# Attention kernel on one core: probability blocks through DRAM, two stores and four loads a head

## The chip, the cores and the metric

The kernel runs on one core of one Trainium2 chip. The metric is the device time of one execution in microseconds. Before the change three timed executions took 833.21, 831.81 and 833.38 us; their median is 833.21 us.

A core has a TensorE (PE) for matrix products, a VectorE (DVE), a ScalarE (ACT) and a GpSimd (POOL), and a SyncE (SP) that here issues every DMA. Each engine runs its own instructions in order and waits on semaphores for the others. A DMA is issued in SP's queue and lands later.

## The reference, cut to what matters

One layer of cross attention and one linear layer with 4-bit weights and a low-rank addition. There are 8 batches (B) of 128 queries and 128 keys, width 512, 32 heads (H) of 128.

```python
x = rmsnorm(layernorm(x)) * ln_weight
q, k, v = x @ w_q.T, ctx @ w_k.T, ctx @ w_v.T        # 32 heads of 128
score = einsum('bqhd,bkhd->bhqk', q, k) + position_bias
score = where(mask, softmax(where(mask, score, -inf)), 0)
x = x0 + layernorm(x0) + einsum('bhqk,bkhd->bqhd', score, v) @ w_out.T
h = layernorm(x)
out = x + h @ W.T + 2 * (h @ W_a @ W_b)              # W decoded from 4-bit codes
```

## The kernel before, in words

Every large product is made from operands split into a high and a low part (fp32r), three products for one, on PE (line 1184). After a setup, in which head 0's scores are made too, a loop of seven passes and an unrolled eighth treats four heads a pass (G = 4, functions odd_head and even_head of each engine); the last head, 31, stands behind it. All orders are written out by hand.

One head h goes through these steps. PE makes the scores of 8 batches into the banks s_ps (line 1220). DVE adds the bias and takes the maximum (lines 992, 994). ACT takes the exponential with a sum (line 652) into p_blocks, whose free axis is ordered as block of 32 keys, batch, key within the block. DVE makes a factor for each row (lines 999, 1001), ACT multiplies by it (normalise, line 603). DVE then transposes every 32x32 block in place (turn_blocks, line 1009, two instructions of 128x512; p_turned_done counts them).

For `pT`, the probabilities with keys on the partitions, the blocks must also change places: block row i, column k goes to row k, column i. That is the work of `move_blocks` on SP (line 342), 16 DMAs of 32 partitions by 1 KB within SBUF. When they have landed (pT_loaded), PE uses pT for the attention of head h while it is at head h+1 (attend, line 1226). Since pT is single, the move waits until the attention of head h-1 is done (attn_done); since p_blocks is single, ACT waits for the whole move before the exponential of the next head (the wait on pT_loaded in `exps`, at the first half).

Head 0 goes another way before the loop. ACT writes its exponentials ordered by batch (by_batches, the same memory under the name last_pT). PE transposes the 8 tiles with the identity (line 1326), between the two halves of head 1's queries, and DVE copies the result into pT (line 1087). DVE's last step of the first split, of ctx_sum[3] into ctx_lo (split_first 7, line 895), stands ahead of that copy. PE waits for it (`ctx_lo_done, SPLITS`) before it enters the loop with the scores of head 1.

At the end, head 31 is transposed by PE as well; its ACT copy into last_pT, which is the memory of p_blocks, waits for the move of head 30.

SP's queue holds, behind each move, the loads of later weights: k_raw and wo_raw for the next pair of heads, q_raw for head h+3, pos_raw for head h+2, and in the second head of each pass the storing of a decoded slice and the loading of the next.

Of the kernel before, what the change touches and what calls it, by code (L numbers as in the profile page):

```python
# [6 lines left out]
P = 128  # L7
B = 8
# [3 lines left out]
H = 32  # L12
# [6 lines left out]
HB = B // 2  # L19
Q = 32  # L20
# [41 lines left out]
SPLITS = 8  # L62

EARLY_LORA = 3
TURN_BEFORE = (5, 7)
FFN_TRANSPOSE_BEFORE = 5
WARM_UP = 4
# [11 lines left out]
def halves(h):  # L79
    return range(h * HB, (h + 1) * HB)  # L80
# [15 lines left out]
def xattn_ffn(nc, x_d, ctx_d, mask_d, lnw_d, q_d, k_d, pos_d, wo_d, wv_d, codes_d, absmax_d, wa_d, wb_d, out_d):  # L96
    lora_d = nc.dram_tensor("lora_dram", (GROUPS, P, SLICE), f32, kind="Internal").ap()
    ffn_d = nc.dram_tensor("ffn_dram", (GROUPS, P, SLICE), f32, kind="Internal").ap()
    with ExitStack() as ctx:
        def sb(name, shape, dt=f32):  # L100
            return ctx.enter_context(nc.sbuf_tensor(name, shape, dt))

        def sem(name):
            return ctx.enter_context(nc.semaphore(name))
# [134 lines left out]
        decode_moved = sem("decode_moved")  # L239
        ffn_loaded = sem("ffn_loaded")  # L240
        last_ffn_loaded = sem("last_ffn_loaded")
        pT_loaded = sem("pT_loaded")
        stored = sem("stored")

# [35 lines left out]
        p_done = sem("p_done")  # L280
        p_turned_done = sem("p_turned_done")
        turned = sem("turned")
        first_turned = sem("first_turned")
        last_pT_done = sem("last_pT_done")
        attn_done = sem("attn_done")
        attn_hi_done = sem("attn_hi_done")
# [28 lines left out]
        def _(sp):  # L315
# [20 lines left out]
                sp.wait_ge(decoded, g + 1)  # L336
                sp.dma_start(ffn_d[g], level[:, :]).then_inc(decode_moved, 16)

            def move_blocks(keys):
                for k in keys:  # L340
                    for i in range(NQ):
                        sp.dma_start(pT[Q * k:Q * (k + 1), i, :, :],  # L342
                                     p_blocks[Q * i:Q * (i + 1), k, :, :]).then_inc(pT_loaded, 16)

            sp.dma_start(wa, wa_d).then_inc(lora_loaded, 16)
            sp.dma_start(wb, wb_d).then_inc(lora_loaded, 16)
# [30 lines left out]
            load_q(2)  # L377
            sp.wait_ge(bias_done, 1)
            load_pos(2, 0)
            sp.wait_ge(q_lo_done, 3)  # L380
            load_q(3)

# [2 lines left out]
            def group(g, last):  # L385
                for j in range(1, G if last else G + 1):
                    h = G * g + j
                    final = last and j == G - 1
                    m = 2 * g + (j + 1) // 2
                    if j == 1:  # L390
                        if last:

                            sp.wait_ge(wv_lo_done, PRODUCTS * GROUPS)
                            sp.wait_ge(decode_moved, 80 * (GROUPS - 1) + 64)
                            sp.dma_start(wv_raw[:, 0:C - 1, :].rearrange("p c (g s) -> p (c g) s", g=2),
                                         ffn_d[0:2 * (C - 1)].rearrange("g p s -> p g s")).then_inc(ffn_loaded, 16)
                        else:
                            sp.wait_ge(wv_lo_done, PRODUCTS * (g + 1))
                            sp.dma_start(wv_raw[:, :, :], wv_d[g + 1]).then_inc(wv_loaded, 16)
                    if not (last and j + 2 >= G):  # L400
                        sp.wait_ge(bias_done, h + 1)
                        load_pos(h + 2, j % 2)
                    if not final:
                        sp.wait_ge(p_turned_done, 2 * h + 1)
                        sp.sem_inc(sp_passed, 1)
                        sp.wait_ge(attn_done, 2 * h)
                        move_blocks((0, 1))
                        sp.wait_ge(p_turned_done, 2 * h + 2)
                        move_blocks((2, 3))
                    if j % 2 and not last:  # L410
                        sp.wait_ge(k_lo_done, PRODUCTS * (m + 1))
                        load_k(m + 1)
                    if j == 1 or (j == 3 and not last):
                        for i in range(2):
                            sp.wait_ge(wo_lo_done, h + i)
                            load_wo(h + 1 + i, i)
                    if not last:
                        sp.wait_ge(q_lo_done, h + 3)
                        load_q(h + 3)
                        if j == 2:  # L420
                            store_ffn(g)
                            load_codes(g + 1)
                    elif j == 2:
                        store_ffn(g)
                        sp.wait_ge(decode_moved, 80 * GROUPS)
                        sp.dma_start(wv_raw[:, C - 1, :].rearrange("p (g s) -> p g s", g=2),
                                     ffn_d[2 * (C - 1):2 * C].rearrange("g p s -> p g s")).then_inc(last_ffn_loaded, 16)
# [173 lines left out]
        def _(act):  # L601
# [44 lines left out]
            def exps(h, hf, out):  # L646
                act.wait_ge(max_done, 2 * h + hf + 1)
                if hf == 0 and out is by_blocks and not (isinstance(h, int) and h == 0):

                    act.wait_ge(pT_loaded, 16 * NQ * NQ * h)  # L650
                for b in halves(hf):
                    e = act.activation(out(b), p[:, b, :].rearrange("p (k c) -> p k c", c=Q), ACT.Exp,  # L652
                                       bias=neg_max[:, b:b + 1], accum_out=prob_sum[:, b:b + 1])
# [1 line left out]

            def by_blocks(b):
                return p_blocks[:, :, b, :]

            def by_batches(b):
                return last_pT[:, b, :].rearrange("p (k c) -> p k c", c=Q)  # L660

            def in_place(b):
                return p[:, b, :].rearrange("p (k c) -> p k c", c=Q)
# [102 lines left out]


            for hf in range(2):
                exps(0, hf, by_batches)
            for hf in range(2):  # L770
                normalise(0, hf, by_batches)
            act.wait_ge(lora_stored, 16 * C)
            copy_first_values(6)
            copy_first_values(7)
# [85 lines left out]
            for i in range(2):  # L860
                split_wo(i, PAIRS, last_wo_hi)

            act.wait_ge(pT_loaded, 16 * NQ * NQ * (H - 1))
            for hf in range(2):
                act.wait_ge(turned, hf + 1)
                copy(last_pT[:, hf * HB:(hf + 1) * HB, :], s_ps[hf][:, :, :]).then_inc(last_pT_done, 1)
# [26 lines left out]
        def _(dve):  # L893
# [184 lines left out]
            scale_rows(0, 0)  # L1078
            residual(HB)
            scale_rows(0, 1)  # L1080
            for b in range(HB + 1, B):
                residual(b)
            split_first(7, ctx_lo[:, 4, :, :], ctx_sum[3], ctx_hi[:, 4, :, :])

            for hf in range(2):
                dve.wait_ge(first_turned, hf + 1)
                dve.tensor_copy(pT[:, :, hf * HB:(hf + 1) * HB, :],
                                s_ps[hf][:, :, :].rearrange("p b (i c) -> p i b c", c=Q)).then_inc(pT_loaded, 8 * NQ * NQ)
            dve.sem_inc(p_turned_done, 2)
            split_q(2)  # L1090

            def odd_head(g, j, last):
# [84 lines left out]
        def _(pe):  # L1177
# [141 lines left out]
            scores(0, 1)  # L1319
            for b in (6, 7):  # L1320
                first_values(b)
            queries(1, 0, next_queries[0])
            for hf in range(2):
                pe.wait_ge(p_done, hf + 1)
                for i, b in enumerate(halves(hf)):
                    t = pe.transpose(s_ps[hf][:, i, :], last_pT[:, b, :], ident[:, :])
                t.then_inc(first_turned, 1)
            queries(1, 1, next_queries[1])

            pe.wait_ge(ctx_lo_done, SPLITS)  # L1330
            pe.wait_ge(pT_loaded, 16 * NQ * NQ)

            def odd_head(g, j, last):

# [10 lines left out]
                key_product(m, 1, key_slot(j, 1))  # L1345
                if j == 1:
                    pe.wait_ge(values_added, 2 * ADDS * (g + 1))
                pe.wait_ge(pT_loaded, 16 * NQ * NQ * h)
                for hf in range(2):
                    pe.wait_ge(biased, 2 * h + hf + 1)  # L1350
                    attend(j - 1, hf, s_flat(hf), moved)
# [14 lines left out]
            def even_head(g, j, last):  # L1366
# [8 lines left out]

                pe.wait_ge(keys_copied, COPIES * (m + 1))
                queries(h + 1, 0, query_bank(j, 0))
                pe.wait_ge(pT_loaded, 16 * NQ * NQ * h)
                for hf in range(2):
                    pe.wait_ge(biased, 2 * h + hf + 1)  # L1380
                    attend(j - 1, hf, s_flat(hf), moved)
# [39 lines left out]
            for b in range(B):  # L1421
# [11 lines left out]
                if b >= 4:  # L1433
                    pe.wait_ge(out_added, B * (PAIRS - 2) + b - 3)
                output(b, wo_hi, wo_lo)
            pe.wait_ge(pT_loaded, 16 * NQ * NQ * (H - 1))
            for hf in range(2):
                attend(G - 2, hf, w_ps[hf][:, :], moved)
                pe.wait_ge(last_pT_done, hf + 1)
# [67 lines left out]
```

## Time and profile before

| | before |
|---|---|
| median of three | 833.21 us |
| lowest, highest | 831.81, 833.38 us |
| profiled execution | 831.71 us |
| its span | 829.9 us |
| PE busy | 824.1 us, 99% |
| POOL busy | 535.3 us, 65% |
| DVE busy | 447.5 us, 54% |
| ACT busy | 445.6 us, 54% |
| share of the DMA queue's packets | 24.9% |
| granted TensorE clock | 1.00 |

The span is the time from the first to the last instruction of the program; the execution has 1.8 us around it. A row of the timeline has the start in us from the span's start, the length in us, the engine, the line, the operation, the tile written and the tiles read, the shapes, how many were merged, and in brackets the idle time ahead of it with what ended it. Matmul rows overlap: the pace is the distance between starts, not the length.

### The profile page before, as it was taken

Reading aid. Unit: us, or ns where it says so; the run is one execution under the profiler, and the core shown is the slowest. Engines: PE = TensorE matmul, PEld = TensorE weight load, DVE = VectorE, ACT = ScalarE, POOL = GpSimd, SP = SyncE. Lnnn points to the kernel's source line nnn. Section 1 sums busy time; section 2 is a strip of 40 time slices with the busy share of each in tenths; the row PEclk is TensorE's granted clock in tenths of the full one; section 3 lists DMA queues with packets and bytes.
Section 4 is the critical chain, followed back from the end, with each engine's and each line's share of the span. In section 5 each row is a group of like instructions: output and inputs, shape, how many; then the busy total and the mean of one; then the engine's idle time right before and its main releaser. Section 6 shows DMA issues by size and latency. Waiting matters only on the chain.

```text
span 829.9 us, 15761 instructions
## 1 busy us (share of the span) xinstructions
PE 824.1 (99%) x4702; PEld 720.3 (87%) x4702; DVE 447.5 (54%) x754; ACT 445.6 (54%) x1297; POOL 535.3 (65%) x556
## 2 busy tenths in 40 slices
PE   9999999999999999999999999999999999999998
PEld 6888888988899888988889888998889888898886
DVE  5785655355634656245553556346562455636683
ACT  5766474464726555364644647355553646447632
POOL 0576778467875778756785578757787567855440
PEclk9999999999999999999999999999999999999999
DMA  8212332122211323113221222113230232311102
GB/s 326 90 42 90 107 94 68 54 92 66 93 36 58 98 68 97 26 69 98 79 89 54 92 66 92 38 55 97 69 96 24 71 98 68 104 41 51 46 13 89
DMA packets 50357, 64.46 MB, mean 78 GB/s; under 512 B 10752, under 2 KB 36480, under 8 KB 49312
## 3 DMA queue, kind: packets, MB, share of 16 engines
q1 hardware_dynamic: 50336, 64.20, 24.9%
q8 instruction: 10, 0.16, 0.1%
q14 instruction: 11, 0.09, 0.0%
HBM read 44.24 MB, written 4.19 MB: 58 GB/s over the span
## 4 chain that ended last, share of the span: by engine, by line
PE 94%; DVE 2%; ACT 2%; SPq 1%; DMA 0%; issue 0%; POOL 0%; POOLq 0%; ACTq 0%
PE w_ps L1184 44%; PE o_ps L1184 35%; PE s_ps L1220 6%; PE s_ps L1226 6%; SPq L342 1%; ACT p_blocks L652 1%; DVE stats L901 1%; DVE resid L1017 1%; PE s_ps L1184 1%; ACT p_blocks L603 1%; PE s_ps L1250 0%; PE o_ps L1250 0%; PE w_ps L1286 0%; PE w_ps L1241 0%; PE w_ps L1247 0%; DMA pT<-p_blocks 0%
## 5 line engine op out<-in xcount | busy, mean ns | idle before, releaser
L531 POOL TENSOR_SCALAR picked<-codes 128x256 f32<-128x256 int32 x112 | 124.3, 1110 | 19.2 <-POOL level L534 15.6
L496 POOL TENSOR_TENSOR p<-pos_raw,mask_add 128x1024 f32<-128x1024 f32 x32 | 69.6, 2175 | 103.1 <-ACT p_blocks L652 102.8
L652 ACT ACTIVATE p_blocks<-p,neg_max 128x128 f32<-128x128 f32 x248 | 96.1, 389 | 48.4 <-DVE neg_max L994 44.0
L534 POOL TENSOR_TENSOR level<-level,picked 128x256 f32<-128x256 f32 x112 | 90.6, 809 | 20.9 <-POOL picked L531 20.9
L468 POOL TENSOR_TENSOR ring_lo<-k_raw,ring_hi 128x256 fp32r<-128x256 f32 x105 | 76.5, 740 | 30.2 <-ACT ring_hi L603 27.3
L603 ACT ACTIVATE ring_hi<-k_raw 128x256 fp32r<-128x256 f32 x105 | 38.8, 414 | 101.0 <-POOL k_raw L458 101.0
L1017 DVE TENSOR_TENSOR resid<-o_ps,resid 128x512 f32<-128x512 f32 x102 | 68.7, 686 | 44.7 <-PE o_ps L1184 44.5
L1184 PE MATMUL w_ps<-ctx_hi,ring_hi 128*128 128x512 f32 x210 | 84.7, 403 | 0.0
L1184 PE MATMUL w_ps<-ctx_hi,ring_lo 128*128 128x512 f32 x210 | 82.1, 391 | 0.0
L1184 PE MATMUL w_ps<-ctx_lo,ring_hi 128*128 128x512 f32 x210 | 81.7, 389 | 0.0
L603 ACT ACTIVATE p_blocks<-p_blocks,row_scale 128x128 f32<-128x128 f32 x248 | 77.2, 391 | 1.1 <-DVE row_scale L1001 1.1
L1184 PE MATMUL o_ps<-wo_hi,attn_hi 128*128 128x512 f32 x180 | 70.2, 390 | 0.0
L1184 PE MATMUL o_ps<-wo_hi,attn_lo 128*128 128x512 f32 x180 | 70.1, 389 | 0.0
L1184 PE MATMUL o_ps<-wo_lo,attn_hi 128*128 128x512 f32 x180 | 70.0, 389 | 0.0
L992 DVE TENSOR_TENSOR p<-s_ps,p 128x512 f32<-128x512 f32 x62 | 42.5, 686 | 41.8 <-PE s_ps L1220 41.8
L1220 PEld LDWEIGHTS s_ps<-kT,qT 128*128 128x128 f32 x496 | 59.8, 191 | 1.9
L1220 PE MATMUL s_ps<-kT,qT 128*128 128x128 f32 x496 | 60.4, 275 | 0.0
L1226 PEld LDWEIGHTS s_ps<-pT,v 128*128 128x128 f32 x480 | 58.2, 191 | 2.3
L1009 DVE STREAM_TRANSPOSE p_blocks<-p_blocks 128x512 f32<-128x512 f32 x60 | 39.1, 691 | 36.7 <-ACT p_blocks L603 36.7
L1226 PE MATMUL s_ps<-pT,v 128*128 128x128 f32 x480 | 58.4, 275 | 0.0
L895 DVE TENSOR_TENSOR attn_lo<-s_ps,attn_hi 128x512 fp32r<-128x512 f32 x62 | 40.9, 680 | 31.1 <-ACT attn_hi L603 31.1
L984 DVE TENSOR_TENSOR v<-w_ps,v 128x512 f32<-128x512 f32 x21 | 14.5, 692 | 76.7 <-PE w_ps L1184 76.7
(229 smaller groups left out, 2289.8 us busy)
## 6 DMA issues: line engine op xcount, KB each, us to landing
pT<-p_blocks SPq DMA_DIRECT2D x480, 32.0 KB, 1.8
k_raw<-k_dram SPq DMA_DIRECT2D x16, 512.0 KB, 3.5
wv_raw<-wv_dram SPq DMA_DIRECT2D x8, 1024.0 KB, 4.8
q_raw<-q_dram SPq DMA_DIRECT2D x32, 256.0 KB, 3.7
wo_raw<-wo_dram SPq DMA_DIRECT2D x32, 256.0 KB, 4.0
resid<-x_dram SPq DMA_DIRECT2D x2, 1024.0 KB, 12.6
pos_raw<-pos_dram SPq DMA_DIRECT2D x32, 64.0 KB, 3.8
out_dram<-resid SPq DMA_DIRECT2D x8, 256.0 KB, 2.0
```

What stands on the lines that cost most here:

```text
L468: return pool.tensor_tensor(out, whole, hi.bitcast(f32), ALU.subtract)
L496: pool.tensor_tensor(p[:, :, :], pos, mask_add[:, :, :], ALU.add).then_inc(bias_done, 1)
L531: then(pool.tensor_scalar((level if code == 0 else picked)[:, :], codes[:, :], float(code), NF4[code], match, ALU.mult))
L534: then(pool.tensor_tensor(level[:, :], level[:, :], picked[:, :], ALU.add))
L603: return act.activation(out, in_, ACT.Copy, **kw)
L652: e = act.activation(out(b), p[:, b, :].rearrange("p (k c) -> p k c", c=Q), ACT.Exp, bias=neg_max[:, b:b + 1], accum_out=prob_sum[:, b:b + 1])
L895: return dve.tensor_tensor(out, whole, hi.bitcast(f32), ALU.subtract)
L992: dve.tensor_tensor(p[:, bs, :], banks[hf][:, :, :], p[:, bs, :], ALU.add).then_inc(biased, 1)
L1017: dve.tensor_tensor(resid[:, b, :], bank, resid[:, b, :], ALU.add).then_inc(out_added, 1)
L1184: mm = pe.matmul(out, l, r, start=opens and i == 0, stop=closes and i == n - 1, skip_group_check=True)
L1220: s = pe.matmul(banks[hf][:, i, :], qT[:, at], kT[:, slot, at], start=True, stop=True)
L1226: o = pe.matmul(out[:, i * L:(i + 1) * L], v[:, b, j * DH:(j + 1) * DH], by_keys(b), start=True, stop=True)
```

## The change

The stores write p_blocks, two columns of blocks at a time, into a new DRAM tensor blocks_dram; the loads read it back with the block index on the other side, one load for each 32 partitions of pT, all four block columns at once. SP waits for a store's landing (blocks_stored, one semaphore for each pair) before it loads from it. ACT's wait in `exps` and at the end is now for the two stores. Head 0 goes the same way: its exponentials are written by blocks, DVE turns them (turn_blocks(0), ahead of three residual steps and the last split), SP moves them; PE's 8 transposes and DVE's two copies are gone.

```diff
+STORE = 16
+LOADS = 16 * NQ
+    blocks_d = nc.dram_tensor("blocks_dram", (2, P, 2, B, Q), f32, kind="Internal").ap()
-            def move_blocks(keys):
-                for k in keys:
-                    for i in range(NQ):
-                        sp.dma_start(pT[Q * k:Q * (k + 1), i, :, :],
-                                     p_blocks[Q * i:Q * (i + 1), k, :, :]).then_inc(pT_loaded, 16)
+            def move(h):
+                first = isinstance(h, int) and h == 0
+                for pair in range(2):
+                    sp.wait_ge(p_turned_done, 2 * h + pair + 1)
+                    if pair == 0 and not first:
+                        sp.sem_inc(sp_passed, 1)
+                        sp.wait_ge(pT_loaded, LOADS * h)
+                    sp.dma_start(blocks_d[pair], p_blocks[:, 2 * pair:2 * pair + 2, :, :]).then_inc(blocks_stored[pair], STORE)
+                if not first:
+                    sp.wait_ge(attn_done, 2 * h)
+                    sp.sem_inc(sp_passed, 1)
+                for pair in range(2):
+                    sp.wait_ge(blocks_stored[pair], STORE * (h + 1))
+                    for k in range(2):
+                        at = 2 * pair + k
+                        sp.dma_start(pT[Q * at:Q * (at + 1), :, :, :],
+                                     blocks_d[pair, :, k, :, :].rearrange("(i r) b c -> r i b c", i=NQ)).then_inc(pT_loaded, 16)
...
             load_pos(2, 0)
+            move(0)
...
-                        sp.wait_ge(p_turned_done, 2 * h + 1)
-                        sp.sem_inc(sp_passed, 1)
-                        sp.wait_ge(attn_done, 2 * h)
-                        move_blocks((0, 1))
-                        sp.wait_ge(p_turned_done, 2 * h + 2)
-                        move_blocks((2, 3))
+                        move(h)
...
-                    act.wait_ge(pT_loaded, 16 * NQ * NQ * h)
+                    for pair in range(2):
+                        act.wait_ge(blocks_stored[pair], STORE * h)
...
-                exps(0, hf, by_batches)
+                exps(0, hf, by_blocks)
...
             scale_rows(0, 1)
+            turn_blocks(0)
             for b in range(HB + 1, B):
                 residual(b)
             split_first(7, ctx_lo[:, 4, :, :], ctx_sum[3], ctx_hi[:, 4, :, :])
-            for hf in range(2):
-                dve.wait_ge(first_turned, hf + 1)
-                dve.tensor_copy(pT[:, :, hf * HB:(hf + 1) * HB, :],
-                                s_ps[hf][:, :, :].rearrange("p b (i c) -> p i b c", c=Q)).then_inc(pT_loaded, 8 * NQ * NQ)
-            dve.sem_inc(p_turned_done, 2)
...
-            queries(1, 0, next_queries[0])
             for hf in range(2):
-                pe.wait_ge(p_done, hf + 1)
-                for i, b in enumerate(halves(hf)):
-                    t = pe.transpose(s_ps[hf][:, i, :], last_pT[:, b, :], ident[:, :])
-                t.then_inc(first_turned, 1)
-            queries(1, 1, next_queries[1])
+                queries(1, hf, next_queries[hf])
             pe.wait_ge(ctx_lo_done, SPLITS)
-            pe.wait_ge(pT_loaded, 16 * NQ * NQ)
+            pe.wait_ge(biased, 2)
...
-                pe.wait_ge(pT_loaded, 16 * NQ * NQ * h)
+                pe.wait_ge(pT_loaded, LOADS * h)
```

PE's order between the halves of head 1's queries and the loop (the branch), before:

```order
L1184 MATMUL w_ps<-xn_hi,q_lo 128x512
L1326 MATMUL s_ps<-ident,p_blocks 128x128 [waits p_done]
L1326 MATMUL s_ps<-ident,p_blocks 128x128 x3
L1326 MATMUL s_ps<-ident,p_blocks 128x128 [waits p_done]
L1326 MATMUL s_ps<-ident,p_blocks 128x128 x3
L1184 MATMUL w_ps<-xn_hi,q_hi 128x512 [waits q_lo_done]
...
L1411 UNCONDITIONAL_BRANCH [waits pT_loaded,ctx_lo_done]
```

and now:

```order
L1193 MATMUL w_ps<-xn_hi,q_lo 128x512
L1193 MATMUL w_ps<-xn_hi,q_hi 128x512 [waits q_lo_done]
L1193 MATMUL w_ps<-xn_lo,q_hi 128x512
...
L1415 UNCONDITIONAL_BRANCH [waits biased,ctx_lo_done]
```

The 8 transposes are gone, and the two waits for p_done; the wait for ctx_lo_done at the loop's entry stays.

DVE's order at the same place, from the second half's row factors on, before:

```order
L999 RECIPROCAL recip<-prob_sum 128x4 [waits exp_done]
L1001 TENSOR_TENSOR row_scale<-recip,row_valid 128x4 [waits recip_done]
L944 TENSOR_SCALAR resid<-resid,ln_scale,ln_shift 128x512 [waits staged] x3
L895 TENSOR_TENSOR ctx_lo<-wv_raw,ctx_hi 128x1024 [waits ctx_hi_done]
L1087 COPY pT<-s_ps 128x4x128 [waits first_turned] x2
L895 TENSOR_TENSOR q_lo<-q_raw,q_hi 128x512 [waits q_hi_done]
```

and now:

```order
L1013 RECIPROCAL recip<-prob_sum 128x4 [waits exp_done]
L1015 TENSOR_TENSOR row_scale<-recip,row_valid 128x4 [waits recip_done]
L1023 STREAM_TRANSPOSE p_blocks<-p_blocks 128x512 [waits p_done]
L1023 STREAM_TRANSPOSE p_blocks<-p_blocks 128x512
L958 TENSOR_SCALAR resid<-resid,ln_scale,ln_shift 128x512 [waits staged] x3
L909 TENSOR_TENSOR ctx_lo<-wv_raw,ctx_hi 128x1024 [waits ctx_hi_done]
L909 TENSOR_TENSOR q_lo<-q_raw,q_hi 128x512 [waits q_hi_done]
```

Two transposes of blocks with a wait for p_done now stand ahead of the three residual steps and of the split into ctx_lo; the two copies into pT are gone.

SP's order in a head of the loop, before:

```order
L342 DMA pT<-p_blocks 32x256 [waits p_turned_done,attn_done]
L342 DMA pT<-p_blocks 32x256 x7
L408 REGISTER_ALU
L342 DMA pT<-p_blocks 32x256 [waits p_turned_done]
L342 DMA pT<-p_blocks 32x256 x7
```

and now:

```order
L353 DMA blocks_dram<-p_blocks 128x512 [waits pT_loaded]
L348 REGISTER_ALU
L353 DMA blocks_dram<-p_blocks 128x512 [waits p_turned_done]
L358 REGISTER_ALU [waits attn_done]
L361 DMA pT<-blocks_dram 32x4x256 [waits blocks_stored0]
L361 DMA pT<-blocks_dram 32x4x256
L361 DMA pT<-blocks_dram 32x4x256 [waits blocks_stored1]
L361 DMA pT<-blocks_dram 32x4x256
```

Six issues stand where sixteen stood, with two waits for a landing among them. Head 0's six stand in the same order ahead of the loop.

## Rows read from the trace of the kernel before

**Rows 1.** The page, part 1: busy us, share of the span, instructions.
```profile
PE 824.1 (99%) x4702; PEld 720.3 (87%) x4702; DVE 447.5 (54%) x754; ACT 445.6 (54%) x1297; POOL 535.3 (65%) x556
```

**Rows 2.** The waits of PE: us in total, times, longest us.
```profile
PE w_ps L1247 <- POOL ident L447: 1.6, 1, 1.6
PE o_ps L1220 <- ACT qT L603: 0.7, 1, 0.7
PE o_ps L1184 <- DVE xn_lo L895: 0.4, 1, 0.4
```

**Rows 3.** The timeline of PE, head 0's transposes to its attention: start, length.
```profile
58.46 0.40 PE L1184 MATMUL w_ps<-xn_hi,q_lo 128*128 128x512 f32 x1
58.69 1.04 PE L1326 MATMUL s_ps<-ident,p_blocks 128*128 128x128 f32 x8
59.49 0.47 PE L1184 MATMUL w_ps<-xn_hi,q_hi 128*128 128x512 f32 x1
59.80 0.39 PE L1184 MATMUL w_ps<-xn_lo,q_hi 128*128 128x512 f32 x1
...
62.34 2.01 PE L1220 MATMUL s_ps<-kT,qT 128*128 128x128 f32 x16
...
66.94 1.95 PE L1226 MATMUL s_ps<-pT,v 128*128 128x128 f32 x16
```

**Rows 4.** The timeline of DVE, at head 0, head 1 and head 30.
```profile
54.62 1.99 DVE L1001 TENSOR_TENSOR row_scale<-recip,row_valid 128x4 f32<-128x4 f32 x1
56.54 1.45 DVE L944 TENSOR_SCALAR resid<-resid,ln_scale,ln_shift 128x512 f32<-128x512 f32 x3
57.91 1.22 DVE L895 TENSOR_TENSOR ctx_lo<-wv_raw,ctx_hi 128x1024 fp32r<-128x1024 f32 x1
...
71.86 1.30 DVE L1009 STREAM_TRANSPOSE p_blocks<-p_blocks 128x512 f32<-128x512 f32 x2 [1.96 <-ACT p_blocks L603]
...
763.99 0.69 DVE L994 TENSOR_REDUCE neg_max<-p 128x4 f32<-128x512 f32 x1
```

**Rows 5.** The timeline of ACT, at head 0, head 2 and head 30.
```profile
56.65 1.28 ACT L603 ACTIVATE p_blocks<-p_blocks,row_scale 128x128 f32<-128x128 f32 x4 [1.10 <-DVE row_scale L1001]
...
84.39 0.40 ACT L652 ACTIVATE p_blocks<-p,neg_max 128x128 f32<-128x128 f32 x1 [2.37 <-DMA pT<-p_blocks]
...
764.99 0.40 ACT L652 ACTIVATE p_blocks<-p,neg_max 128x128 f32<-128x128 f32 x1 [2.02 <-DMA pT<-p_blocks]
```

**Rows 6.** The timeline of POOL at head 0.
```profile
54.46 2.14 POOL L496 TENSOR_TENSOR p<-pos_raw,mask_add 128x1024 f32<-128x1024 f32 x1 [0.80 <-ACT p_blocks L652]
...
60.29 0.74 POOL L458 TENSOR_TENSOR k_raw<-k_raw 128x256 f32<-128x256 f32 x1 [0.18 <-POOL ring_lo L468]
61.21 0.74 POOL L458 TENSOR_TENSOR k_raw<-k_raw 128x256 f32<-128x256 f32 x1 [0.18 <-POOL k_raw L458]
```

**Rows 7.** The timeline of SP's queue, the move of head 1.
```profile
72.66 10.45 SPq L342 DMA_DIRECT2D pT<-p_blocks  x16
```

**Rows 8.** DMA issues: count, KB each, median us to landing.
```profile
pT<-p_blocks SPq DMA_DIRECT2D x480, 32.0 KB, 1.8
...
resid<-x_dram SPq DMA_DIRECT2D x2, 1024.0 KB, 12.6
...
lora<-lora_dram SPq DMA_DIRECT2D x8, 128.0 KB, 3.0
...
ffn_dram<-level SPq DMA_DIRECT2D x8, 128.0 KB, 2.6
```

**Rows 9.** SP's lines 337 and 342: issue ns min/median/max, first and last start.
```profile
L337 SPq DMA_DIRECT2D ffn_dram<-level x8: 364/370/581, 102.1 to 782.2; - x8
L342 SPq DMA_DIRECT2D pT<-p_blocks x480: 508/590/1270, 72.7 to 781.5; - x160
```

**Rows 10.** The timeline of PE at head 2's attention step and at head 31's scores.
```profile
85.74 1.95 PE L1226 MATMUL s_ps<-pT,v 128*128 128x128 f32 x16
...
772.11 1.13 PE L1220 MATMUL o_ps<-kT,qT 128*128 128x128 f32 x8 [0.69 <-ACT qT L603]
```

More of the change, by code:

```diff
@@ L241, in xattn_ffn @@
         last_ffn_loaded = sem("last_ffn_loaded")
+        blocks_stored = [sem(f"blocks_stored{i}") for i in range(2)]
         pT_loaded = sem("pT_loaded")
@@ L282, in xattn_ffn @@
         turned = sem("turned")
-        first_turned = sem("first_turned")
         last_pT_done = sem("last_pT_done")
@@ L657, in by_blocks @@
                 return p_blocks[:, :, b, :]
-            def by_batches(b):
-                return last_pT[:, b, :].rearrange("p (k c) -> p k c", c=Q)
             def in_place(b):
@@ L768, in _ @@
             for hf in range(2):
-                exps(0, hf, by_batches)
+                exps(0, hf, by_blocks)
             for hf in range(2):
-                normalise(0, hf, by_batches)
+                normalise(0, hf, by_blocks)
             act.wait_ge(lora_stored, 16 * C)
@@ L861, in _ @@
                 split_wo(i, PAIRS, last_wo_hi)
-            act.wait_ge(pT_loaded, 16 * NQ * NQ * (H - 1))
+            for pair in range(2):
+                act.wait_ge(blocks_stored[pair], STORE * (H - 1))
             for hf in range(2):
@@ L1377, in even_head @@
                 queries(h + 1, 0, query_bank(j, 0))
-                pe.wait_ge(pT_loaded, 16 * NQ * NQ * h)
+                pe.wait_ge(pT_loaded, LOADS * h)
                 for hf in range(2):
@@ L1435, in _ @@
                 output(b, wo_hi, wo_lo)
-            pe.wait_ge(pT_loaded, 16 * NQ * NQ * (H - 1))
+            pe.wait_ge(pT_loaded, LOADS * (H - 1))
             for hf in range(2):
```

## The prediction

> **What bounds the kernel now.** I read the busy shares first, then the waits of PE, then the timelines of the engines around head 0 and around the last heads, and last what SP issues and when it lands. PE is busy 824.1 us of a span of 829.9 us, the next engine 65% [rows 1]. The list of all that PE waited for has three entries, 1.6, 0.7 and 0.4 us [rows 2]; the first is before the first product of the kernel. So the time is PE's own work, instruction after instruction, and an edit counts in two ways only: by work taken from PE, or by a wait of PE made or removed. No entry names the move of the blocks. Whatever the 16 transfers cost SP, PE has not waited for one in any of the heads. The reader is to see in the timeline of PE that the pace is 0.23 us a product of 512 columns (58.46 to 58.69) and that the rows follow each other without idle time [rows 3].
>
> **Work taken from PE.** The 8 transposes of head 0 start at 58.69 and the next product at 59.49, so 0.80 us; the product behind them takes 0.31 us to the next start (59.49 to 59.80) where others take 0.23 [rows 3]. Together 0.88 us, if nothing takes the place.
>
> **What takes the place: the entrance of the loop.** PE reaches the wait for ctx_lo_done now at 62.34 [rows 3], and the split that it waits for ended at 57.91 + 1.22 = 59.13 [rows 4], 3.2 us early. After the change PE is there at 62.34 - 0.88 = 61.46. DVE is later. The row factors end at 54.62 + 1.99 = 56.61 [rows 4], the normalising of the second half at 56.65 + 1.28 = 57.93 [rows 5], and only then may the turn of the blocks start, 1.30 us for the two by the row at 71.86; then three residual steps, 1.45 us, then the split, 1.22 us [rows 4]. That is 57.93 + 1.30 + 1.45 + 1.22 = 61.90, less about 0.1 for overlaps of rows: 61.8. So PE waits 0.35 us at the least. The split reads two tensors of SBUF, and at that time POOL now works on the key sums, 60.29 to 61.03 and from 61.21 [rows 6]. What such a meeting costs shows at 54.62: DVE's factors of 128x4, an operation with two inputs, took 1.99 us and ended at 56.61, when POOL's bias, 54.46 to 56.60, ended [rows 4, 6]. DVE would be ready for the split at about 60.6, POOL's sum runs until 61.03, so 0.4 us more: the split ends at 62.25 and PE is released near 62.3. I take a wait of 0.8 us. Ends: 0.35 us (no meeting), and 1.6 us (POOL first with both sums, until 61.95). The Trainium skill, "SBUF — State Buffer", on the engine side's shared port, says that DVE's operations with two SBUF inputs and GpSimd's exclude each other for a whole instruction; by that rule the wait is the 0.8, without it the 0.35, and the row of 1.99 us agrees with the rule.
>
> Who is behind the wait: the scores of head 1, and with them DVE's bias, ACT's exponential and all of PE. ACT's queries of head 1 come 0.88 us earlier, so they do not hold the scores. POOL's next sums slip by up to 1 us. Their first use is later by several products, so I count them at nothing.
>
> **Head 0's blocks.** They are needed by PE at 66.94 now [rows 3], that is 66.06 with the transposes gone and 66.9 with the 0.8 us wait. The turn ends at 57.93 + 1.30 = 59.2, SP's second store is issued by 59.2 + 0.1 + 0.37 = 59.7 (0.37 from the store of a decoded slice) [rows 9]. A store to DRAM lands after 2.6 us by the row of ffn_dram [rows 8]: 62.3; the first pair's by 61.7. Four loads follow. An issue costs between 0.37 and 0.59 us [rows 9], so the last is issued between 63.2 and 64.1; it lands after 3.0 us by the row of lora, which has the same 128 KB [rows 8]: 66.2 to 67.1. That is even with 66.9. I take no further wait, as the middle, 66.65, is before it. The ends are 1.8 us a landing as for moves within SBUF [rows 8], which gives 64.7 and nothing to wait for, and issues of 1.27 us [rows 9], which gives 61.7 + 4 x 1.27 + 3.0 = 69.8, a wait of 2.9 us more.
>
> A sentence apart: the Trainium skill, "DMA: Bandwidth & Descriptors", anatomy of one DMA, gives about 2.0 us fixed for each transfer plus its bytes over 436 GB/s (a fit for the GpSimd path), most of it for the receipt of the write, and DRAM as the slowest target; a chain of store and load then pays the fixed part twice, an estimate of 2.6 + 2.3 us, which speaks against this change. By it head 0's blocks would land at about 66.1. The measured 2.6 and 3.0 us say the same, a little more.
>
> **The heads of the loop.** SP issues 16 transfers from 72.66 for 10.45 us, and the last lands 1.8 us later [rows 7, 8]; PE needs them at 85.74 [rows 10]. Now the first store goes at the same time; the second is issued about 0.7 us after the first, lands at about 76.3; the loads are issued by 78.6 and landed by 81.6. The blocks come about 3 us earlier, and SP reaches its loads of weights about 4.5 us earlier. PE was not waiting, so both are worth nothing. ACT waited for the move twice before an exponential: at 84.39 and at 764.99 [rows 5]; now it waits for the stores, long landed. In head 2 PE has no wait behind it (rows 2 name none) and the gain is nothing. At head 30 it is on the path: behind the exponentials and the normalising ACT drains head 31's queries, and PE is idle 0.69 us for them at 772.11 [rows 10]. But the maximum that ACT also needs ended only at 763.99 + 0.69 = 764.68 [rows 4]; ACT would have started near 764.72. The gain is 0.27 us, not 2.02. It can't be under nothing or over 0.69. At the end ACT's copy of head 31 waits for head 30's move; PE used it without a wait, so nothing.
>
> **Sum.** -0.88 + 0.8 - 0.27 = -0.35 us. Against the profiled execution, 831.71 us, that is 831.36. The median is 833.21, and four executions of this kernel (with the profiled one) lie between 831.71 and 833.38 with a mean of 832.53. Median less sum is 832.9, mean less sum 832.2; I take the middle, 832.5 us. What a measurement can tell from no change is about 0.2%, 1.7 us; the sum is a fifth of that.
>
> **The rivals.**
> 1. Head 0's blocks are late and end PE's wait at 66.1 to 66.9, not ctx_lo. For: the two estimates overlap, and two landings stand in a chain where there was none. Price: a landing at 67.1 gives 0.2 us more, at 69.8 2.9 us more; so 832.7 to 835.4, most likely 833.2.
> 2. The change is a clean gain: DVE's split is not delayed by POOL (0.35 us), the blocks are early. -0.88 + 0.35 - 0.27 = -0.8 us, 832.0 us.
> 3. Faster by more than the resolution: PE's 0.88 us are all saved, and both late idle times, 0.69 and 0.4 us [rows 2], vanish since everything arrives early. -1.97 us: 830.8 us. Against it: the 0.4 us at the end wait for DVE's work that has nothing to do with the move, and the maximum at 764.68.
> 4. Slower: the round trip through DRAM is longer than the slack of the heads in the loop. The blocks of an odd head are turned at 71.86 + 1.30 = 73.16 and needed at 85.74, 12.6 us [rows 4, 10]. Issues take 0.4 + 4 x 0.59 = 2.8 us, so the two landings may take 9.8 us together; beyond that each us costs 1 us in 15 heads, and 0.12 us over is already 0.2%. Landings of 12.6 us occur, in the crowd of the first loads [rows 8]; with those it would be 15 x 15 us more. One us over, as a mark: 848 us. Against: in the loop ffn_dram and lora land in 2.6 and 3.0 us, 4 us inside the limit, and the queue's packets fill a quarter of the time.
>
> **How the numbers follow.** Forecast (-0.35) 0.48; rival 1 0.22; rival 2 0.15; rival 3 0.05; rival 4 0.05; something that no row shows, either way, 0.05. All of forecast, 1 up to a landing 1.7 us late, and 2 are within 0.2%; the spread of a median of three (1.6 us between lowest and highest) puts some of them outside. Faster 0.11, same 0.78, slower 0.11. The range, 831.0 to 834.8, takes in the sums from -0.8 to about +1.5 us and that spread; rivals 3 and 4 and the far end of 1 are left out.
>
> **What would show it.** Right: PE has 8 matmuls fewer; a new wait of PE, 0.5 to 1 us, before the first scores of head 1, ended by DVE's ctx_lo; the attention of head 0 starts near 66.9; the moves of a head take SP about 6 us in place of 10.5; ACT has no wait for the move at 84 and 765; PE's wait for ACT's qT near 772 is about 0.4 us. Wrong: PE waits for pT anywhere in the loop; a wait for pT at head 0 of over 1 us; no wait for ctx_lo at all; a PE wait at 772 that is gone or unchanged; a span more than 1.7 us away from 829.5.

## The result

| | before | after |
|---|---|---|
| median of 20 runs each, same chip | 832.52 us | 833.97 us |
| lowest, highest | 831.81, 833.43 | 833.04, 834.53 |
| ratio, 95% interval | | 1.0018 [1.0012, 1.0024] |
| profiled execution: span | 829.9 us | 831.3 us |
| first scores of head 0 to first scores of head 1 | 13.69 us | 15.01 us |

The change makes the kernel slower by 1.45 us, with 1.0 to 2.0 us inside the interval. The forecast was 832.5 us, no change. Against the 832.52 us of before in these runs the sum of the prediction, -0.35 us, was off by 1.8 us.

The page after, part 1, against [rows 1]:

```profile
PE 823.6 (99%) x4694; PEld 720.0 (87%) x4694; DVE 451.2 (54%) x754; ACT 445.8 (54%) x1297; POOL 535.9 (64%) x556
```

PE has 8 matmuls fewer and 0.5 us less work, and the span is longer: it waits. The waits of PE after, against [rows 2]:

```profile
PE s_ps L1229 <- DVE ctx_lo L909: 2.1, 1, 2.1
PE w_ps L1256 <- POOL ident L462: 1.6, 1, 1.6
PE o_ps L1229 <- ACT qT L618: 0.4, 1, 0.4
PE o_ps L1193 <- DVE xn_lo L909: 0.4, 1, 0.4
```

The first is new, and it is the wait that the prediction named, at 2.1 us in place of 0.8. The third is the one at head 31's scores, down from 0.7 to 0.4 as forecast. No wait is for pT. The timeline of PE after, against [rows 3] (line 1229 is the scores, line 1235 the attention):

```profile
61.70 0.39 PE L1193 MATMUL w_ps<-xn_hi,q_lo 128*128 128x512 f32 x1
64.17 2.05 PE L1229 MATMUL s_ps<-kT,qT 128*128 128x128 f32 x16 [2.08 <-DVE ctx_lo L909]
...
68.81 1.95 PE L1235 MATMUL s_ps<-pT,v 128*128 128x128 f32 x16
```

From the last product to the scores it is 2.47 us where 0.23 would do: a loss of 2.24 us. The timeline of DVE after, against [rows 4]:

```profile
58.48 1.31 DVE L1023 STREAM_TRANSPOSE p_blocks<-p_blocks 128x512 f32<-128x512 f32 x2 [1.35 <-ACT p_blocks L618]
59.71 2.30 DVE L958 TENSOR_SCALAR resid<-resid,ln_scale,ln_shift 128x512 f32<-128x512 f32 x3
61.93 1.78 DVE L909 TENSOR_TENSOR ctx_lo<-wv_raw,ctx_hi 128x1024 fp32r<-128x1024 f32 x1
```

The three residual steps took 2.30 us where they had taken 1.45, the split 1.78 where it had taken 1.22. What GpSimd did at that time, against [rows 6]:

```profile
59.89 0.92 POOL L483 TENSOR_TENSOR ring_lo<-k_raw,ring_hi 128x256 fp32r<-128x256 f32 x1 [2.78 <-ACT ring_hi L618]
60.99 0.74 POOL L473 TENSOR_TENSOR k_raw<-k_raw 128x256 f32<-128x256 f32 x1 [0.18 <-POOL ring_lo L483]
61.91 0.72 POOL L473 TENSOR_TENSOR k_raw<-k_raw 128x256 f32<-128x256 f32 x1 [0.18 <-POOL k_raw L473]
62.59 1.70 POOL L483 TENSOR_TENSOR ring_lo<-k_raw,ring_hi 128x256 fp32r<-128x256 f32 x1
```

GpSimd works through all of it, and its own key splits are longer as well, 0.92 and 1.70 us where they take 0.74. The chain of waits of the stretch, up to PE's scores at 64.17; each line has the start, the length and the piece of work:

```profile
58.48 1.31 DVE p_blocks L1023 x2
59.79 2.22 DVE resid L958 x3
62.01 1.71 DVE ctx_lo L909
63.72 0.44 issue
```

The chain runs through DVE for 5.2 us and has 0.44 us between DVE's end and PE's first product, in which PE's queue starts again. The moves themselves went well. SP's queue at head 1 after, against [rows 7], and what they took to land, against [rows 8]:

```profile
74.00 0.81 SPq L353 DMA_DIRECT2D blocks_dram<-p_blocks  x2
76.04 1.74 SPq L361 DMA_DIRECT2D pT<-blocks_dram  x4
```

```profile
blocks_dram<-p_blocks SPq DMA_DIRECT2D x62, 256.0 KB, 2.2
pT<-blocks_dram SPq DMA_DIRECT2D x124, 128.0 KB, 2.6
```

SP is done 3.8 us after it began, where it had taken 10.45 us. The differences along the two profiles: the setup up to the first scores of head 0 is 0.51 us longer (48.65 and 49.16), from there to head 1's scores it is +1.32 us, from there to head 31's scores -0.45 us (62.34 to 772.11, and 64.17 to 773.49), and the rest is equal. The 0.51 us are no part of the change: two further executions of the same changed kernel have 47.97 there (experiment 7).

### The profile page after: what moved, and what is told of

It is laid out like the page before. It is cut to its first block, busy times and chain, and to the rows that moved or that the text cites. A ratio compares the mean times of both kernels' runs of the same rounds, so it can differ in the third digit from the quotient of the medians.

```text
span 831.3 us, 15555 instructions
## 1 busy us (share of the span) xinstructions
PE 823.6 (99%) x4694; PEld 720.0 (87%) x4694; DVE 451.2 (54%) x754; ACT 445.8 (54%) x1297; POOL 535.9 (64%) x556
## 3 DMA queue, kind: packets, MB, share of 16 engines
HBM read 60.49 MB, written 20.45 MB: 97 GB/s over the span
## 4 chain that ended last, share of the span: by engine, by line
PE 95%; DVE 3%; ACT 1%; issue 0%; POOL 0%; POOLq 0%
PE w_ps L1193 45%; PE o_ps L1193 35%; PE s_ps L1229 6%; PE s_ps L1235 6%; ACT p_blocks L668 1%; DVE stats L915 1%; DVE resid L1031 1%; PE s_ps L1193 1%; PE s_ps L1259 0%; ACT p_blocks L618 0%; PE o_ps L1259 0%; PE w_ps L1295 0%; DVE ctx_lo L909 0%; DVE resid L958 0%; PE w_ps L1250 0%; PE w_ps L1256 0%
## 6 DMA issues: line engine op xcount, KB each, us to landing
resid<-x_dram SPq DMA_DIRECT2D x2, 1024.0 KB, 12.3
```

## The experiments

All ratios are to the kernel before in the same runs. The edits are to the changed kernel.

**1. The split ahead of the turn.**

```diff
             scale_rows(0, 1)
+            split_first(7, ctx_lo[:, 4, :, :], ctx_sum[3], ctx_hi[:, 4, :, :])
             turn_blocks(0)
             for b in range(HB + 1, B):
                 residual(b)
-            split_first(7, ctx_lo[:, 4, :, :], ctx_sum[3], ctx_hi[:, 4, :, :])
```

> The changed kernel with DVE's last split into ctx_lo put ahead of the turn of head 0's blocks, and the three residual steps behind it. Theory A (the time was lost by PE's wait for ctx_lo at the loop's entrance, 2.24 us from product to product, because DVE does the turn, three residual steps and only then the split): the wait is gone, head 0's blocks start as early as before, and what stays is the work taken from PE, -0.88 us, and -0.27 us at head 30: 1.1 us under the kernel before, ratio 0.9986. Rival B (the loop pays for the way through DRAM, and the wait only takes the place of another that would come): the time stays at 1.0 to 1.5 us over the kernel before, with a wait of PE for pT or k_lo in place of the one for ctx_lo.

Measured: 830.59 us, ratio 0.9984 [0.9975, 0.9993]. The waits of PE:

```profile
PE w_ps L1256 <- POOL ident L462: 1.6, 1, 1.6
PE o_ps L1229 <- ACT qT L618: 0.4, 1, 0.4
PE o_ps L1193 <- DVE xn_lo L909: 0.4, 1, 0.4
```

The wait for ctx_lo is gone and nothing has taken its place; DVE used the 1.4 us in which it waited for the normalising. The three residual steps still take 2.30 us there, but now nobody waits for them. This is theory A: 1.1 us under the kernel before expected, 1.4 us measured (832.01 in these runs). The order of the steps turns a loss into a gain.

**2. The loop alone through DRAM.** Head 0 by PE's transposes and DVE's copies as in the kernel before; the copies also tell the semaphores of the stores.

```diff
-            move(0)
...
-            turn_blocks(0)
...
+            for hf in range(2):
+                dve.wait_ge(first_turned, hf + 1)
+                dve.tensor_copy(pT[:, :, hf * HB:(hf + 1) * HB, :],
+                                s_ps[hf][:, :, :].rearrange("p b (i c) -> p i b c", c=Q)).then_inc(pT_loaded, LOADS // 2)
```

> Only the loop's moves go through DRAM; head 0 goes as in the kernel before (8 transposes on PE, copies by DVE). Theory A: the loop's part is worth -0.27 us at head 30 and nothing else, ratio 0.9997, PE's wait for qT 0.4 us instead of 0.7. Rival B: the loop's part is what costs, +1 us or more, ratio 1.0012 or more.

Measured: 831.47 us, ratio 0.9995 [0.9986, 1.0004]. PE's wait for qT is 0.4 us. The loop's part costs nothing and gains at most what was expected; rival B, 1.0012 or more, is outside the interval.

**3. Head 0 alone through DRAM.** The loop's 16 transfers back in place of the stores and loads.

```diff
+                if not first:
+                    sp.wait_ge(p_turned_done, 2 * h + 1)
...
+                            sp.dma_start(pT[Q * k:Q * (k + 1), i, :, :],
+                                         p_blocks[Q * i:Q * (i + 1), k, :, :]).then_inc(pT_loaded, 16)
```

> Only head 0 goes through DRAM; the loop moves its blocks by 16 transfers within SBUF as in the kernel before. Theory A: -0.88 us of transposes and +2.24 us of the wait for ctx_lo, so +1.4 us, ratio 1.0016, and PE waits 2.1 us before the first scores of head 1. Rival B: -0.9 to 0 us, since the costly part is not in it.

Measured: 834.08 us, ratio 1.0026 [1.0015, 1.0037], so +2.1 us. The waits of PE:

```profile
PE s_ps L1238 <- DVE ctx_lo L918: 2.1, 1, 2.1
PE o_ps L1238 <- ACT qT L629: 1.1, 1, 1.1
```

The whole loss is here, and the expected 1.4 us lie inside the interval. 0.4 us of the rest show in the second row: with the moves within SBUF head 31's scores waited 1.1 us, where the kernel before waited 0.7. The last 0.3 us are not explained; the clock does not show in them, since the three executions with a granted clock of 1.0 (median 834.06 us) are level with the five at 0.997 or 0.998 (834.13). Experiments 2 and 3 together settle which part of the change costs.

**4. GpSimd held back until the split is made.**

```diff
             make_bias(1)
+            pool.wait_ge(ctx_lo_done, SPLITS)
             start_of_pair(1, 1)
```

> The changed kernel, with GpSimd's first key split and key sums of the first pair held back until DVE has made the last split into ctx_lo. Theory A2 (DVE's residual steps and its split are stretched by GpSimd's work at the same time, 2.30 us for 1.45 and 1.78 for 1.22): they take 1.45 and 1.22 us again, ctx_lo is done 1.4 us earlier, and the whole is 1.3 us under the changed kernel, about level with the kernel before (ratio 1.0000), if the key splits, 2.5 us later, still come before their products. Rival (the lengths have another cause, such as the stores of the blocks that read SBUF at that time): the two lengths stay and so does PE's wait, ratio 1.0018 or more.

Measured: 834.52 us, ratio 1.0035 [1.0021, 1.0049]. The timeline of DVE:

```profile
59.32 1.42 DVE L959 TENSOR_SCALAR resid<-resid,ln_scale,ln_shift 128x512 f32<-128x512 f32 x3
60.66 1.22 DVE L910 TENSOR_TENSOR ctx_lo<-wv_raw,ctx_hi 128x1024 fp32r<-128x1024 f32 x1
```

The theory on the lengths holds: with GpSimd idle they are 1.42 and 1.22 us, although SP's stores of the blocks run at that time as before. The time did not follow. PE's two waits, and two of the products behind them:

```profile
62.32 1.15 PE L1230 MATMUL s_ps<-kT,qT 128*128 128x128 f32 x8 [0.64 <-DVE ctx_lo L910]
64.69 1.95 PE L1230 MATMUL s_ps<-kT,qT 128*128 128x128 f32 x8 [1.22 <-ACT qT L619]
66.87 0.63 PE L1194 MATMUL w_ps<-ctx_lo,ring_hi 128*128 128x512 f32 x1
67.30 0.63 PE L1194 MATMUL w_ps<-ctx_hi,ring_lo 128*128 128x512 f32 x1
```

ACT's draining of head 1's queries stands behind its copy of GpSimd's late key sum, and PE waited 1.22 us for it: my sentence "if the key splits still come before their products" had looked past the copy. Then the products ran at 0.43 us instead of 0.23. The stretches of PE there (the number after the engines' busy times is the granted clock):

```profile
64.00:66.20 2.20, 1.51 (x7) 1.51 (x8) 1.01 (x2) 1.16 (x3) 2.02 (x3) 0.70 0.00 0
66.20:68.50 2.30, 2.30 (x9) 1.86 (x8) 2.23 (x4) 1.84 (x8) 1.49 (x3) 0.55 0.46 132
```

The granted clock fell to the lower level, 1.2 GHz for 2.4, after two waits of together 1.9 us. All five executions of this kernel have a mean clock of 0.998.

**5. The split between the turn and the residual steps.**

```diff
             turn_blocks(0)
+            split_first(7, ctx_lo[:, 4, :, :], ctx_sum[3], ctx_hi[:, 4, :, :])
             for b in range(HB + 1, B):
                 residual(b)
-            split_first(7, ctx_lo[:, 4, :, :], ctx_sum[3], ctx_hi[:, 4, :, :])
```

> The changed kernel with DVE's order turn, split into ctx_lo, residual steps (instead of turn, residual steps, split). Theory A (PE waits for ctx_lo alone): the split ends about 61.0, before PE arrives at 61.9, and the time is that of the first experiment, 1.1 us under the kernel before, ratio 0.9986. Theory A3 (an operation of DVE with two SBUF inputs holds up a GpSimd operation, and ACT stands in order behind GpSimd): the split, 59.7 to 60.9, pushes GpSimd's key split of 59.89 to 60.9, its first key sum to 62.6, ACT's copy of it to 63.0 and ACT's draining of head 1's second half of queries to 63.5; PE then waits about 0.8 us for qT before the second four scores, in place of any wait for ctx_lo: 0.3 us under the kernel before, ratio 0.9996.

Measured: 831.47 us, ratio 0.9989 [0.9980, 0.9998]. DVE and GpSimd:

```profile
58.91 1.18 DVE L909 TENSOR_TENSOR ctx_lo<-wv_raw,ctx_hi 128x1024 fp32r<-128x1024 f32 x1
60.02 2.77 DVE L958 TENSOR_SCALAR resid<-resid,ln_scale,ln_shift 128x512 f32<-128x512 f32 x3
```

```profile
59.09 1.60 POOL L483 TENSOR_TENSOR ring_lo<-k_raw,ring_hi 128x256 fp32r<-128x256 f32 x1 [2.77 <-ACT ring_hi L618]
```

This time DVE began first and kept its length, and GpSimd's operation was the one stretched: its 0.74 us became 1.60, ending 0.6 us behind the end of the split at 60.09. The effect on PE is that of A3, a wait for qT, but of 0.4 us and not 0.8:

```profile
62.59 1.16 PE L1229 MATMUL s_ps<-kT,qT 128*128 128x128 f32 x8 [0.40 <-ACT qT L618]
```

The ratio stands between the two expectations and cannot tell them apart; the row can.

**6. PE's wait moved behind the branch.**

```diff
-            pe.wait_ge(ctx_lo_done, SPLITS)
             pe.wait_ge(biased, 2)
...
                 pe.wait_ge(attn_lo_done, 2 * (h - 1) + 2)
+                if j == 1:
+                    pe.wait_ge(ctx_lo_done, SPLITS)
                 scores(h, 0)
```

> The changed kernel, with PE's wait for ctx_lo_done moved from the branch at the loop's entrance to the place just before the scores in the loop body. DVE is as late as before. Theory A4 (PE starts 0.46 us after DVE's end instead of 0.05 to 0.13 as behind other waits because the branch and what follows it come after the wait): the wait shrinks from 2.08 to about 1.75 us, 0.35 us under the changed kernel, ratio 1.0014. Rival (the restart costs 0.4 us wherever the wait stands): the wait stays 2.1 us, ratio 1.0018.

Measured: 833.71 us, ratio 1.0016 [1.0007, 1.0025]. The split ended at 61.48 + 1.78 = 63.26 and PE began at 63.51:

```profile
61.48 1.78 DVE L909 TENSOR_TENSOR ctx_lo<-wv_raw,ctx_hi 128x1024 fp32r<-128x1024 f32 x1
```

```profile
63.51 2.75 PE L1229 MATMUL s_ps<-kT,qT 128*128 128x128 f32 x16 [1.88 <-DVE ctx_lo L909]
```

The restart took 0.25 us where it took 0.46. So about 0.2 us of it go with the place of the wait, at the branch; this rests on one profile, and the other half is not explained. In this execution the clock fell behind the wait (products at 0.43 us), and the interval of the ratio holds both expectations, so the time can't show 0.2 us.

**7. The changed kernel twice more.** No edit.

> The changed kernel as it is, one more profiled execution. Theory C (PE's wait of 2.1 us at the loop's entrance is close to what makes the granted clock fall, so that some executions pay for it twice): either as in the first profile (clock 1.0 throughout, first scores of head 1 to the attention of head 0 4.64 us) or a stretch of 3.4 us at half clock behind the wait, and that distance 6.2 us. Rival: the clock never falls there.

> As the one before, a third profiled execution of the changed kernel, with the same two outcomes: 4.64 us and clock 1.0, or 6.2 us with 3.4 us at half clock.

Measured: 833.54 and 833.47 us, spans 831.8 and 831.7 us. In both the clock fell. Scores and attention of the first of them, and its stretch behind the wait:

```profile
62.97 3.68 PE L1229 MATMUL s_ps<-kT,qT 128*128 128x128 f32 x16 [2.08 <-DVE ctx_lo L909]
...
69.25 1.95 PE L1235 MATMUL s_ps<-pT,v 128*128 128x128 f32 x16
```

```profile
62.00:64.00 2.00, 1.03 (x5) 1.04 (x6) 1.64 (x2) 0.04 (x1) 1.82 (x2) 0.77 0.50 151
64.00:66.00 2.00, 2.00 (x11) 2.00 (x11) 0.88 (x2) 0.72 (x2) 1.20 (x3) 0.50 0.38 140
```

Against the first profile of the same kernel:

```profile
62.00:64.00 2.00, 0.08 (x1) 0.00 (x0) 2.00 (x3) 1.24 (x3) 2.00 (x2) 1.00 0.67 205
64.00:66.00 2.00, 1.83 (x17) 1.84 (x17) 1.37 (x2) 0.55 (x2) 1.25 (x2) 1.00 0.37 68
```

69.25 - 62.97 = 6.28 us in place of 68.81 - 64.17 = 4.64: the same wait of 2.08 us costs 1.6 us more in two of three executions. In these two the setup was 1.19 us shorter (head 0's scores at 47.97 for 49.16), so the spans differ by 0.4 to 0.5 us only.

The record has the mean granted clock of each execution, and it tells how often this happens. A fall like this one loses 1.7 us (the clock is 0.77, 0.50 and 0.87 in the three stretches of 2 us from 62 to 68), 0.002 of 832 us, and so shows as 0.998. Of the 20 executions of the changed kernel in the result 16 have 0.998. The other four, at 0.999 and 1.0, are also the four fastest: their median is 833.31 us against 834.16, and the profiled execution, 833.04 us, is one of them. Over all the kernels in which PE waits 1.9 us or more there, in one wait or two (the changed kernel and experiments 3, 4 and 6) 35 of 46 executions have 0.998 or 0.997. Of the 135 executions on record with a clock without such a wait (72 of the kernel before, 63 of experiments 1, 2, 5, 9 and the stores twice and four times) none is under 0.999.

**8. The stores twice, four times, six times.** Each repetition waits for the one before; the kernel is that of experiment 1.

```diff
+                    for again in range(N):
+                        for pair in range(2):
+                            sp.wait_ge(blocks_stored[pair], ...)
+                            sp.dma_start(blocks_d[pair], p_blocks[:, 2 * pair:2 * pair + 2, :, :]).then_inc(blocks_stored[pair], STORE)
```

> The kernel of the first experiment, with both stores of each head of the loop issued a second time, one after the other has landed, before the loads: the chain of a move gets 2.7 us longer (a store's issue and landing). Theory A (the blocks of an odd head land 5.8 us, those of an even head 8.4 us before PE needs them): no change, ratio 0.9984 as the first experiment, although 16 MB more are written. Rival B (the loop is sensitive to the traffic or to the time of the move): 0.5 us or more slower than the first experiment.

Measured: 830.63 us, ratio 0.9977 [0.9968, 0.9986], against 830.59 us of experiment 1: no change.

> As the one before, with the stores issued four times in all: 8.1 us more in the chain of a move. Theory A: the blocks of an odd head are now 2.3 us late, in 15 heads, those of an even head just in time: 15 x 2.3 = 35 us slower than the first experiment, ratio about 1.04, with waits of PE on pT. Rival B (the slack is larger, since SP's and the landings' times overlap): under 10 us slower.

Measured: 830.91 us, ratio 0.9988 [0.9978, 0.9998], no wait of PE on pT in the list. My 35 us were wrong, since I had the repetition at 2.7 us; SP's queue at head 1 shows what it takes:

```profile
73.56 6.64 SPq L358 DMA_DIRECT2D blocks_dram<-p_blocks  x6
80.50 2.22 SPq L365 DMA_DIRECT2D pT<-blocks_dram  x4
```

The two pairs overlap. From the first store to the first load it is 8.98 us at head 1 (71.52 to 80.50), where experiment 1 has 2.05 (72.38 to 74.43), so three repetitions took 6.9 us there; at head 2 they took 6.1 us (8.13 us for 2.04), and so in most heads. Only at head 1 did PE's step with the blocks come late, 0.49 us after the product before it where 0.23 is the pace:

```profile
84.27 0.39 PE L1197 MATMUL w_ps<-xn_hi,q_lo 128*128 128x512 f32 x1
84.76 2.05 PE L1239 MATMUL s_ps<-pT,v 128*128 128x128 f32 x16
```

In the other odd heads it came on the pace. So 6.1 us more in a move are not yet too much; the next expectation, which has the odd heads "just in time", reads too little slack out of this.

> The kernel of the first experiment with the stores of each head of the loop issued six times in all, each after the one before has landed. With four times SP took 2.04 us a repetition and the blocks of odd heads were just in time. Theory A (the slack then was nothing for odd heads, 2.7 us for even ones): two more repetitions, 4.1 us, make the blocks late by 4.1 us in 15 heads and by 1.4 us in 15: about 80 us slower than the first experiment, 60 to 110, with PE waiting for pT. Rival B (something else gives way, such as DVE and ACT shifting with PE so that the move starts later too): under 30 us.

Measured, one execution: 894.76 us, 64 us over experiment 1. The waits of PE:

```profile
PE s_ps L1239 <- DMA pT<-blocks_dram: 44.1, 16, 4.2
PE w_ps L1239 <- DMA pT<-blocks_dram: 1.0, 1, 1.0
```

Within the expected 60 to 110, but not as it was made up: PE waited in 17 places, not 30, for 45 us, the longest 4.2 us. These are the 15 odd heads, most of them with 2.0 to 3.0 us, and heads 10 and 30. Five repetitions make a move of an odd head 10.2 us longer (at head 9 it is 13.97 us from the first store to the end of the last load's issue, in experiment 1 3.79), and PE waited about 2.6 us of them, so the slack of an odd head is about 7.5 us, an estimate from these rows. The other 19 us go with a granted clock of 0.981 over the 893 us, the lower level after the waits: 0.019 x 893 = 17 us.

**9. The first drain earlier at head 30,** on top of experiment 1.

```diff
                 for hf in range(2):
                     normalise(h, hf, by_blocks)
+                    if last and hf:
+                        drain_q(h + 1, 0, query_bank(j, 0))
                     attention(2 * (h - 1) + hf, j - 1, hf, s_flat(hf))
```

> The kernel of the first experiment, and in head 30 ACT drains the first half of head 31's queries before the second attn_hi copy instead of after it. Theory A (PE's 0.42 us at head 31's scores are a wait for the first drain, which stands 0.5 us later in ACT's order than it has to): the wait is gone, 0.45 us under the first experiment, ratio to the kernel before 0.9978 to 0.9980. Rival (the second drain, or DVE's maximum behind it, takes its place): the same as the first experiment.

Measured: 830.48 us, ratio 0.9979 [0.9970, 0.9988]. The scores of head 31 start without a wait:

```profile
770.02 1.13 PE L1232 MATMUL o_ps<-kT,qT 128*128 128x128 f32 x8
```

The profile shows the gain (from head 30's scores 9.16 us, in experiment 1 9.65), the ratios 0.9979 and 0.9984 do not separate the two. It is the fastest version by its ratio: 1.9 us under the kernel before, 3.3 us under the changed one, from the medians over before in each comparison (-1.89 and +1.45).

## Why the prediction was wrong

The step that failed is the second term of the sum, "I take a wait of 0.8 us" at the loop's entrance, and with it the far end of that term: "1.6 us (POOL first with both sums)" was below the 2.24 us lost (its own rows give 1.7: 61.95 + 1.22 against 61.46). The mechanism was right in place, engine and cause: PE waits for ctx_lo because DVE's turn and residual steps stand ahead of the split, shown by experiment 1, which removes it, and by 2 and 3, which put the whole loss at head 0.

The size was off, in three pieces. Against the forecast end of the split, 61.8 without any meeting, shifted by the 0.5 us of the setup to 62.3, it ended at 63.71, 1.4 us later: 0.85 us in the residual steps (2.30 for 1.45) and 0.56 us in the split (1.78 for 1.22). Experiment 4 gives back both. The prediction had counted 0.4 us for a meeting of the split with GpSimd and nothing for the residual steps, because it looked only for operations with two SBUF inputs; a TENSOR_SCALAR reads one tensor and its two columns of factors and was stretched as well. Why it is stretched no run here shows. The trace of the kernel before had both signs:

```profile
44.66 2.58 DVE L944 TENSOR_SCALAR resid<-resid,ln_scale,ln_shift 128x512 f32<-128x512 f32 x4
59.38 0.74 POOL L468 TENSOR_TENSOR ring_lo<-k_raw,ring_hi 128x256 fp32r<-128x256 f32 x1 [2.78 <-ACT ring_hi L603]
```

Four residual steps took 2.58 us beside GpSimd's decoding in the setup, where three alone took 1.45. And GpSimd's work began not with the key sum at 60.29 but with a key split at 59.38, just when the residual steps would start. The third piece is the restart of PE at the branch, 0.46 us from DVE's end where I had allowed 0.05; experiment 6 gives 0.2 us of it to the place of the wait.

With the term at its measured size the sum is -0.88 + 2.24 - 0.27 = +1.09 us, which is inside 1.0 to 2.0 us. The prediction also had no term for the clock. In the result the four executions without the fall are 0.8 us over the kernel before and the 16 with it 1.6 us, so part of the 1.45 us goes with the clock. The 0.8 us between them is half of what the fall cost in the profiles, 1.6 us; the setup differed by 1.2 us the other way between those executions, and that is not settled.

Point by point. *PE's 0.88 us*: right; the distance from the last product of the first half to the wait is shorter by the transposes, and experiment 1 has the gain. *Head 0's blocks*: right that they are no wait. The loads went out from 61.27 to 63.03, landed after 2.6 us, 65.6, and were needed at 68.81, not near 66.9. In experiment 1, without the long wait, there is no PE wait for them either. *The loop*: right. SP's move takes 3.8 us and not 6, and the slack of an odd head, said to be 4 us in landings, is about 7.5 us; rival 4 was right in that a move beyond it costs in the 15 odd heads, and in that this point is far off. *Head 30*: right, 0.7 us fell to 0.4. *The end*: no wait. *Rival 1* did not happen, *rival 2* is what experiment 1 makes of the change (with the wait itself gone), *rival 3* did not happen.

The chances gave slower 0.11 and same, meant as within 0.2%, 0.78. The 1.0018 is within 0.2%, but 20 executions of each kernel tell it from no change; the prediction had taken the resolution from three. The case "the wait at the entrance is larger" had no chance: its far end was put at 1.6 us, and with -0.88 and -0.27 that is +0.45 us. The range, 831.0 to 834.8, does contain 833.97; what failed is the sign. Of its own signs of being wrong one came: the span, 831.3 us, is 1.8 us from 829.5.

## What to carry to other kernels

When work is taken from the engine that bounds the kernel, ask which wait it now reaches earlier, and when something is put ahead of that wait's releaser, look for an order in which the releaser goes first; here one step put ahead of two others is worth 2.9 us (+1.45 and -1.42 against the kernel before). Give an operation that lands beside GpSimd's work the length that the same operation has beside GpSimd's work elsewhere in the trace, not the one it had alone. And where nobody waits for a transfer, its time is worth nothing: here SP's share of a move fell from 10.45 to 3.8 us without a gain, and the stores could be issued four times without a loss that the times show. Its slack, not its time, is the number to read.

## What the runs showed of the hardware

A wait of PE of about 2 us was followed by a stretch at the lower clock in some executions and not in others of the same kernel, with the same wait: three profiles, two with it, 1.6 us each; by the mean clock 16 of the 20 executions of the result have it. DVE's TENSOR_SCALAR of 128x512 in fp32, three in a row, took 1.42 to 1.45 us with GpSimd idle and 2.30 to 2.77 us with GpSimd at work on SBUF, and GpSimd's own operation of 0.74 us took up to 1.70 us there. A store of 256 KB from SBUF to DRAM landed in 2.2 us and a load of 128 KB from it in 2.6 us, so the way through DRAM, 2 stores and then 4 loads of 1 KB pieces, was quicker than 16 transfers within SBUF: 6.4 us from the first issue to the last landing (74.00 to 77.78, and 2.6) for 12.3 (10.45 and 1.8), since 16 issues take SP's queue 10.45 us. Writing 16 MB more (HBM written 4.19 MB before, 20.45 MB after) slowed nothing that the traces show; with the stores four times it is 67.63 MB, and the time 830.91 us for 830.59.
